# A fused cross-attention, self-attention and expert kernel: self-attention with compact probabilities, scores for the 32x32 diagonal blocks alone, and counters per bank

## What is computed

```python
x = x + xattn(layernorm(x), ctx, Wq, Wk, Wv, Wo, gq, gk)   # 16 heads of 128, 257 keys a sequence
x = x + attn(layernorm(x), w_qkv, w_proj, q_gain)          # the layer that is changed
x = x + moe(layernorm(x), Wg, W1, W3, W2, sw1, sw3, sw2)   # 8 experts, top 1, one shared
# attn: 16 query heads and 4 key heads of 16, ternary weights, a root mean square norm and
# rotary embedding on q and k, causal softmax over the 32 tokens of a sequence, a root mean
# square norm of y over its 256 numbers, then the projection w_proj:
qkv = ternary_linear(x, w_qkv)
q, k = apply_rotary_emb(rms_norm(q)), apply_rotary_emb(rms_norm(k));  q = q * q_gain
y = softmax(causal(q @ k.T * 16 ** -0.5)) @ v
out = ternary_linear(rms_norm(y.reshape(..., 256)), w_proj)
```

## Time and profile before

| | |
|---|---|
| runs | 1604.68, 1611.82 (median), 1613.89 us |
| profiled execution | 1609.09 us; 1607.3 us from the first to the last instruction |
| busy in it | TensorE 1378.4 us (86%), VectorE 1044.2 (65%), ScalarE 864.9 (54%), GpSimd 540.7 (34%) |
| granted TensorE clock, mean | 0.946 |

### The profile page before, as it was taken

One profiled execution on the slowest core, in us unless ns is written; L12 is line 12 of the kernel. 1 busy time (PEld: TensorE's weight loads), 2 busy tenths in 40 slices (PEclk: granted clock), 3 DMA queues, 4 the chain that ended last, 5 costly groups with the idle time before them and its releaser, 6 DMA issues.

```text
span 1607.3 us, 32866 instructions
## 1 busy us (share of the span) xinstructions
PE 1378.4 (86%) x9178; PEld 956.8 (60%) x9178; DVE 1044.2 (65%) x3905; ACT 864.9 (54%) x3432; POOL 540.7 (34%) x1338
## 2 busy tenths in 40 slices
PE   5859989998989898989999998989898989955882
PEld 2635757565756666665757565756666665734661
DVE  6836767676767676777767676767676777733112
ACT  5455656566565656565565566565656565621110
POOL 2143333334243525243343334342525243300003
PEclk9989999999999999999998999999999999976896
DMA  9010000000000001010000000000101010100544
GB/s 372 4 28 8 26 17 21 13 27 13 24 17 14 27 10 30 10 30 7 24 17 21 13 25 15 24 17 10 30 10 30 7 33 3 59 6 19 163 127 134
DMA packets 41190, 59.63 MB, mean 37 GB/s; under 512 B 5094, under 2 KB 35953, under 8 KB 40096
## 3 DMA queue, kind: packets, MB, share of 16 engines
q1 hardware_dynamic: 36880, 50.73, 9.9%
q0 software_dynamic: 2064, 6.14, 1.2%
q10 hardware_dynamic: 2176, 2.10, 0.4%
HBM read 48.62 MB, written 10.49 MB: 37 GB/s over the span
## 4 chain that ended last, share of the span: by engine, by line
PE 57%; issue 14%; POOL 10%; DVE 9%; ACT 7%; DMA 3%; POOLq 1%; SPq 0%; DVEq 0%; ACTq 0%
PE AB L587 30%; PE Eb L587 9%; PE Db L587 5%; PE C L720 3%; PE C L587 3%; ACT px L1003 2%; DMA ctxn<-expert_rows 2%; POOL prob L1140 2%; PE AB L783 2%; POOL c_lo L1105 2%; PE C L704 2%; DVE sc L1509 1%; ACT AB L924 1%; POOL c_hi L1103 1%; POOL pjunk L1099 1%
## 5 line engine op out<-in xcount | busy, mean ns | idle before, releaser
L924 ACT ACTIVATE AB<-AB 128x128 f32<-128x128 f32 (+1 forms) x1160 | 302.8, 261 | 180.8 <-PE AB L587 175.8
L1099 POOL TENSOR_TENSOR pjunk<-pjunk 128x1 f32<-128x1 f32 x288 | 55.9, 194 | 703.2 <-DVE sinv L1443 341.3
L1281 DVE BATCH_NORM_STATS2 kst<-AB 128x6 f32<-128x256 f32 x512 | 182.1, 417 | 71.3 <-PE AB L587 64.9
L587 PE MATMUL AB<-wk_hi,c_hi 128*128 128x512 f16 x512 | 205.2, 401 | 20.8 <-DVE sc L1509 10.0
L924 ACT ACTIVATION_READ_ACCUMULATOR AB<-AB 128x1 f32 (+1 forms) x1160 | 215.4, 186 | 0.0
L587 PE MATMUL AB<-wk_lo,c_hi 128*128 128x512 f16 x512 | 204.0, 398 | 0.0
L587 PE MATMUL AB<-wk_hi,c_lo 128*128 128x512 f16 x512 | 203.0, 396 | 0.0
L993 ACT ACTIVATE prob<-prob,nbias,rq 128x257 f32<-128x257 f32 x256 | 150.6, 590 | 39.8 <-DVE nbias L1438 39.4
L1140 POOL TENSOR_SCALAR prob<-prob,sinv 128x257 f32<-128x257 f32 x256 | 123.8, 484 | 20.1
L587 PE MATMUL AB<-ctxT,qpT 128*128 128x257 f32 x512 | 127.3, 392 | 0.2 <-DVE kst L1281 0.2
L962 ACT CAST pT<-C 128x1024 f16<-128x1024 f32 x64 | 64.5, 1008 | 80.4 <-PE C L720 80.4
(11 more groups left out here) (253 smaller groups left out, 3240.7 us busy)
## 6 DMA issues: line engine op xcount, KB each, us to landing
ctxT<-in_ctxT SPq DMA_DIRECT2D x64, 128.5 KB, 2.1
ctxn<-in_ctxn SPq DMA_DIRECT2D x64, 128.0 KB, 2.1
wq_hi<-in_w SPq DMA_DIRECT2D x4, 768.0 KB, 4.9
wq_lo<-in_w SPq DMA_DIRECT2D x4, 768.0 KB, 6.2
expert_rows<-base POOLq DMA_DIRECT2D x1, 2048.0 KB, 15.7
xin<-in_x SPq DMA_DIRECT2D x16, 128.0 KB, 2.2
prob<-in_wqT SPq DMA_DIRECT2D x1, 2048.0 KB, 19.1
xres<-in_x SPq DMA_DIRECT2D x16, 128.0 KB, 2.0
```

Of the source, the lines that this page charges most:

```text
L587: return pe.matmul(out, lhsT, rhs, start=start, stop=stop)
L924: ins = nc.scalar.activation(k, k, ACT.Square, accum_out=sums[0:m, h:h + 1])
L1099: own.mark(pool.tensor_tensor(pjunk[:, 0:1], pjunk[:, 1:2], pjunk[:, 1:2], ALU.mult))
L1281: ins = V.bn_stats(stats[:, 0, 2 * half + n], AB[0:m, 2 + half, 2 * D * n:2 * D * (n + 1)])
```

## The change

- Scores: 64 products of 32 by 32 (one for each head and sequence), each on its own part of the array by rows and columns, into the first 128 columns of the four banks of `AB`; TensorE first waits for all of the banks (`sc_open` and `pv_open` are counters that nobody waits for). The mask is one operation a bank.
- One exponential of 128x512 into `ex`. New step `sm` on VectorE: sums, reciprocal, product, and a transpose of 32x32 blocks into `exT`. `pt` and its drains go.
- `pv`: 16 products of 32 by 32 rows and 128 columns into the four banks, which give y already transposed, padded from 16 to 32 rows a head; ScalarE copies it to `yT` and squares it; `ys` on VectorE adds the squares, `st` is a product with ones that sums over partitions, `yv` scales. `yt` goes. `pr` has four products, with `wproj` padded (`wpad`, at the start).
- `C` becomes two slots `4` and `5` with counters of their own: `rk`, `pt`, `qk`, `up` fill and drain bank by bank, the drains are two operations for one.
- `o{b}` takes the high halves' products first and waits for the low halves behind them, `f` and `Q` likewise.
- `newton` has one operation less. The clearing of `px` on GpSimd goes.
- The order lists of all four engines are written anew.

```diff
-    "PE": """K0 pt3 K1 K2 X K3 o3 Q f rk0 K4 xt1 K5 qkv QP K6 qk s0 rk1 sc K7 s1 pt pv pt0 s2 yt pr rk2 o0 pt1
-              xt2 s3 lg up pos o1 rk3 pt2 dn o2""".split(),
-    "ACT": """K0 ph3 K1 K2 X tl3 K3 oh3 Q K4 xt1 K5 qkv rk0 QP K6 qk e0 rk1 K7 sc pt e1 ph0 tl0 yt rk2 tl1 ph1 oh0
-              xt2 e2 up oh1 lg rk3 ph2 tl2 e3 oh2""".split(),
-    "DVE": """K0 X K1 dp3 K2 XL K3 do3 KN0 Q RQ f K4 K5 qkv K6 s0 sc K7 i0 s1 pt KN1 pv dp0 i1 pr ln2 s2 dp1 lg i2
-              do0 up pos do1 s3 dn dp2 i3 do2""".split(),
-    "POOL": """h2 h0 h3 h1 n3 X r0 ln1 cl r1 c0 c2 c1 n0 r2 y n1 ln2 c3 r3 n2 scat""".split(),
+    "PE": """K0 K1 pt3 K2 X K3 o3 Q f K4 rk0 xt1 K5 qkv QP K6 qk s0 rk1 sc s1 K7 pt0 pv s2 st pr rk2 o0 pt1 o1
+              xt2 s3 lg up pos rk3 dn pt2 o2""".split(),
+    "ACT": """K0 K1 ph3 K2 X K3 tl3 oh3 Q K4 rk0 xt1 K5 qkv QP K6 qk rk1 e0 sc K7 e1 tl0 pv ph0 rk2 oh0 ph1 tl1
+              xt2 oh1 e2 lg up rk3 ph2 tl2 e3 oh2""".split(),
+    "DVE": """K0 X K1 K2 dp3 XL K3 KN0 Q do3 RQ f K4 K5 qkv K6 s0 i0 sc s1 sm K7 KN1 ys yv i1 dp0 pr ln2 do0 dp1
+              s2 lg do1 i2 up pos s3 dn dp2 do2 i3""".split(),
+    "POOL": """h1 h0 c2 n3 h2 X c3 r0 cl ln1 c0 h3 r1 n0 c1 r2 y n1 ln2 r3 n2 scat""".split(),
...
-SLOTS = {"f": "D", "xt1": "E", "qkv": "D", "qk": "C", "sc": BANKS, "pt": BANKS, "pv": "E", "yt": "D",
-         "pr": "E", "X": "E", "xt2": "D", "Q": BANKS, "lg": "D", "up": "C", "QP": BANKS, "pos": "D", "W0": BANKS, "W1": BANKS,
-         "dn": "E", "M01": BANKS, "M23": BANKS, "tw": "012", "KL": BANKS, "rkl": "C"}
+SLOTS = {"f": "D", "xt1": "E", "qkv": "D", "qk": "45", "sc": BANKS, "pv": BANKS, "st": "D",
+         "pr": "E", "X": "E", "xt2": "D", "Q": BANKS, "lg": "D", "up": "45", "QP": BANKS, "pos": "D", "W0": BANKS, "W1": BANKS,
+         "dn": "E", "M01": BANKS, "M23": BANKS, "tw": BANKS, "KL": BANKS, "rkl": "4"}
 for _b in range(NB):
-    SLOTS |= {f"rk{_b}": "C", f"s{_b}": BANKS, f"pt{_b}": "CD", f"o{_b}": "E"}
+    SLOTS |= {f"rk{_b}": "45", f"s{_b}": BANKS, f"pt{_b}": "45D", f"o{_b}": "E"}
...
-        wproj = sb("wproj", [P, KC, DIM])
+        wproj = sb("wproj", [P, 4, DIM])
...
-        vals = sb("vals", [P, AKV, AD + 1])
+        vals = sb("vals", [P, AKV, SQ])
...
+        ex, wpad, ysq, yred = px[:, 0:4], px[:, 8:16], px[:, 4:8], px[:, 8]
+        exT, yT = pxT[:, 0:4], pxT[:, 4:8]
...
+                for tt, s in enumerate("45"):
                     pe.wait_ge(drained[s].sem, drained[s].turn(p, f"pt{b}"))
-                for tt in range(KT):
                     for g in range(G):
                         ins = pe.transpose(C[:, tt, P * g:P * (g + 1)], prob[:, b, g, P * tt:P * (tt + 1)], ident)
-                ins.then_inc(filled["C"].sem, 1)
+                    ins.then_inc(filled[s].sem, 1)
+                pe.wait_ge(drained["D"].sem, drained["D"].turn(p, f"pt{b}"))
...
                 for tt in range(KT):
+                    pe.wait_ge(ph_ready[tt].sem, ph_ready[tt].at(p, f"ph{b}"))
                     mm(Eb[:], cn_hi[:, b, tt], pT[:, b % 2, 0, tt], start=tt == 0, stop=False)
+                    mm(Eb[:], cn_lo[:, b, tt], pT[:, b % 2, 0, tt], start=False, stop=False)
+                for tt, s in enumerate("45"):
+                    pe.wait_ge(drained[s].sem, drained[s].at(p, f"pt{b}"))
                     mm(Eb[:], cn_hi[:, b, tt], pT[:, b % 2, 1, tt], start=False, stop=False)
-                    mm(Eb[:], cn_lo[:, b, tt], pT[:, b % 2, 0, tt], start=False, stop=False)
+                pe.wait_ge(drained["D"].sem, drained["D"].at(p, f"pt{b}"))
                 mm(Eb[:], cl_rows[:, b], pTl[:, b % 2], start=False).then_inc(filled["E"].sem, 1)
             def step_f(p):
-                pe.wait_ge(drained["E"].sem, drained["E"].at(p, "o3"))
+                pe.wait_ge(oh_ready.sem, oh_ready.at(p, "oh3"))
                 start(p, "f")
                 for h in range(H):
-                    for n, (o, w) in enumerate(((0, wvo_hi), (0, wvo_lo), (1, wvo_hi))):
-                        ins = mm(Db[:, 0:DIM], o_halves[:, o, h], w[:, h], start=(h, n) == (0, 0), stop=(h, n) == (H - 1, 2))
+                    mm(Db[:, 0:DIM], o_halves[:, 0, h], wvo_hi[:, h], start=h == 0, stop=False)
+                    mm(Db[:, 0:DIM], o_halves[:, 0, h], wvo_lo[:, h], start=False, stop=False)
+                pe.wait_ge(drained["E"].sem, drained["E"].at(p, "o3"))
+                for h in range(H):
+                    ins = mm(Db[:, 0:DIM], o_halves[:, 1, h], wvo_hi[:, h], start=False, stop=h == H - 1)
                 ins.then_inc(filled["D"].sem, 1)
...
             def step_sc(p):
-                pe.wait_ge(drained["C"].sem, drained["C"].at(p, "qk"))
-                for m, s in enumerate(BANKS):
+                for s in "45":
+                    pe.wait_ge(drained[s].sem, drained[s].at(p, "qk"))
+                for s in BANKS:
                     pe.wait_ge(drained[s].sem, drained[s].turn(p, "sc"))
-                    rows = slice(32 * m, 32 * m + AD)
...
+                pe.sem_inc(sc_open, 1)
+                for kv in range(AKV):
+                    for b in range(NB):
+                        cols = slice(SQ * b, SQ * (b + 1))
+                        for m, s in enumerate(BANKS):
+                            rows = slice(32 * m, 32 * m + AD)
+                            ins = mm(AB[cols, m, SQ * kv:SQ * (kv + 1)], headsT[rows, kv, cols], headsT[rows, AKV + kv, cols])
+                            if (kv, b) == (AKV - 1, NB - 1):
+                                ins.then_inc(filled[s].sem, 1)
             def step_pv(p):
+                pe.wait_ge(exT_ready.sem, exT_ready.at(p, "h"))
                 start(p, "pv")
-                for n, s in enumerate(BANKS):
-                    pe.wait_ge(drained[s].sem, drained[s].at(p, "pt"))
-                    for h in range(4 * n, 4 * n + 4):
-                        ins = mm(Eb[:, (AD + 1) * h:(AD + 1) * (h + 1)], pxT[:, h], vals[:, h % AKV])
+                pe.sem_inc(pv_open, 1)
+                probs = exT.rearrange("p i (kv q) -> p i kv q", kv=AKV)
+                for kv in range(AKV):
+                    for b, s in enumerate(BANKS):
+                        rows = slice(SQ * b, SQ * (b + 1))
+                        ins = mm(AB[SQ * kv:SQ * (kv + 1), b, 0:P], vals[rows, kv], probs[rows, :, kv])
+                        if kv == AKV - 1:
+                            ins.then_inc(filled[s].sem, 1)
+            def step_pr(p):
+                for s in BANKS:
+                    pe.wait_ge(drained[s].sem, drained[s].at(p, "pv"))
+                start(p, "pr")
+                for i in range(4):
+                    ins = mm(Eb[:, 0:DIM], yT[:, i], wproj[:, i], start=i == 0, stop=i == 3)
                 ins.then_inc(filled["E"].sem, 1)
-            def step_yt(p):
...
+            def step_st(p):
+                pe.wait_ge(yred_ready.sem, yred_ready.at(p, "h"))
+                start(p, "st")
+                mm(Db[:, 0:1], yred, ones[:, 0:1]).then_inc(filled["D"].sem, 1)
...
             def probs_high(p, b):
-                act.wait_ge(filled["C"].sem, filled["C"].at(p, f"pt{b}"))
-                nc.scalar.copy(pT[:, b % 2, 0].rearrange("p t n -> p (t n)"), C[:].rearrange("p a n -> p (a n)"))\
-                    .then_inc(ph_ready.sem, 1)
+                for tt, s in enumerate("45"):
+                    act.wait_ge(filled[s].sem, filled[s].at(p, f"pt{b}"))
+                    nc.scalar.copy(pT[:, b % 2, 0, tt], C[:, tt]).then_inc(ph_ready[tt].sem, 1)
...
             def step_sc(p):
                 act.wait_ge(sc_ready.sem, sc_ready.at(p, "h"))
-                act.wait_ge(px_ready.sem, px_ready.before(p))
...
+                nc.scalar.activation(all_of(ex), all_of(sc[:]), ACT.Exp).then_inc(ex_ready.sem, 1)
...
-            def step_pt(p):
-                for n, s in enumerate("01"):
-                    drain(p, "pt", s, pxT[:, 4 * n:4 * n + 4].rearrange("p h n -> p (h n)"), AB[:, n])
+            def step_pv(p):
+                for b, s in enumerate(BANKS):
+                    act.wait_ge(filled[s].sem, filled[s].at(p, "pv"))
+                    ins = nc.scalar.copy(yT.rearrange("p i (b q) -> p b i q", b=NB)[:, b],
+                                         AB[:, b, 0:P].rearrange("p (i q) -> p i q", q=SQ))
+                    ins.then_inc(drained[s].sem, 1)
+                for s in BANKS:
+                    act.wait_ge(drained[s].sem, drained[s].at(p, "pv"))
+                nc.scalar.activation(all_of(ysq), all_of(yT), ACT.Square).then_inc(ysq_ready.sem, 1)
+            def step_qk(p):
+                for n, s in enumerate("45"):
+                    drain(p, "qk", s, all_of(headsT[:, AKV * n:AKV * (n + 1)]), C[:, n])
...
                 v, w = na[0:rows, 0:n], nb_[0:rows, 0:n]
-                step(V.tensor_scalar(w.bitcast(I32), v.bitcast(I32), 1, None, ALU.logical_shift_right))
-                step(V.tensor_scalar(w.bitcast(I32), w.bitcast(I32), -1.0, MAGIC, ALU.mult, ALU.add))
```

(40 more changed lines are left out.)

179 lines of the change are left out of this document (72 added, 107 removed).

## The result

The changed kernel took 1542.04 us, median of 4 runs (1537.42 to 1546.08), against 1609.78 us for the kernel before, measured beside it (4 runs, 1604.68 to 1613.89). The ratio is 0.958 with an interval of 0.953 to 0.963: 68 us faster, where 50 were forecast.

What follows compares the result with a forecast made beforehand. TensorE was taken as the bound. Stages 37.1 + 9.6 + 35.0 = 81.7, with handovers 82.3, 3.1 us less a period: -46 over 15, last tile -4, 1609 - 50 = 1559, stated as 1560; range 1522 to 1605.

Steps and rivals of the forecast that it cites:

- `sc`, 30 ns a record, 3.8 us: Score products on TensorE: 128 records at 30 ns, 3.8 us for 2.7 before, bounds 13 and 53 ns.
- The rival that decides against the change from 60 ns: Small score products do not overlap: 109 ns a record, 14 us, 1712 us in all; chance 0.11 with weaker forms.
- the 53 ns case: Score records cost 53 to 56 ns as the old tiled ones: +3 us a period, 1605, no change; chance 0.10.
- `pv`, 1.5 us: Products of probabilities and values on TensorE: from 3.5 us to 1.5, at best 0.9.
- `s1` 0.4 idle: TensorE follows the masks bank by bank in `s1`, 686.65 to 688.4, with only 0.4 us idle.
- "I add 0.5" for the clock: Half clock expected after `sc`, on `s1` and `K7`, mostly hidden by VectorE's chain: 0.5 us added to the period.
- `pv` waits 1.4 for `kst`: TensorE before `pv` waits for VectorE's stats of `K7`: 1.4 us, the largest new wait.
- Stage C, 37.1: Period from the end of `K6` to the start of `pt2`: 37.1 us, for 37.64 before.
- Stage A, 9.6, with waits of 1.5 before `K1`: From `pt2` to `pt3`: 9.6 us, about as before, with `K1` now inside and waiting 1.5 for its banks.
- Stage B, 35.0 with 0.4 off the wait for `xn1`: From `pt3` to the end of `K6`: 35.0 us for 37.98, losing `K1`'s 2.6 and 0.4 of the wait.
- The last tile, -4: End of the kernel: shorter self-attention steps save about 9, others add 7, a split saves 2: -4 us.
- The rival of few waits and cheap `sc`: New waits (4.6 us) mostly absent, or score products at their lower bound: period 80, 1525 us; chance 0.17.

Runs made afterwards that it cites:

- wide scores: Changed kernel with the 16 score products of 128 columns and ten masks of before: 1571.53 us, ratio 0.9752.
- Masks first: Changed kernel with `i0` moved behind `sc` in VectorE's list: 1508.91 us, ratio 0.9341.
- the filler: Changed kernel plus six unused full-array products of 512 columns where TensorE waits for the masks: ratio 0.9463.
- `do3` early: Changed kernel with `i0` behind `sc` on VectorE, and `do3` put back ahead of `KN0`: ratio 0.9474.
- same-part kernel: Changed kernel with the 64 small score products reordered, four in a row on the same 32x32 part of the array: 1550.2 us, ratio 0.9618.

## Why the prediction was right, and which terms were off

The time is in the range, the sign and the likeliest case are right, and the period is 82.29 for 82.3. That agreement is partly luck: terms of up to 2.5 us were off and cancelled.

- **`sc`, 30 ns a record, 3.8 us.** Mis-sized: 10 ns, 1.28 us, below my lower bound of 13. I scaled the columns by four from the wide products at 53 ns; but those took 88 ns on average (2.81 us for 32), with four row groups only, while the small ones rotate over sixteen parts. With its four masks the edit is worth -1.5 us a period (wide scores) where the products were charged +1.1. The rival that decides against the change from 60 ns is excluded; I gave it and its weaker forms 0.11, and the 53 ns case 0.10. The trace has a row on either side of the rule in the Trainium skill, "TensorEngine Tiling (Array Packing)", Instruction Overhead (some 60 cycles a matmul, an estimate of 25 ns): 24 ns with four products in a row on one part agrees, 10 ns with neighbours on different parts does not. In the first order the narrow products are longer than the wide ones (3.12 for 2.79 us), in the second less than half.
- **`pv`, 1.5 us.** Measured 0.51, below the 0.9 I gave as the best. `pr` at 1.97 (1.94) and `sm`'s one-pass transpose of 0.71 (0.69) were right; `ys` costs 1.02 for 0.69.
- **`s1` 0.4 idle.** Failed: 1.81. I had `e0` end before `sc` did, at 685.4 against 686.15, "so that `i0` is not late". With `sc` at 1.28 TensorE's scores were ready long before `e0`, and `i0` held the masks 1.4 us beyond them. Masks first shows it. The faster product uncovered the wait that my slow one had hidden.
- **"I add 0.5" for the clock.** Failed. The fall came on `s1` and `K7` as said, and a second time on `s2`, which I had not looked for. Half speed took 2.0 us of TensorE's time a period by the filler and 2.4 by masks first, against one fall in the kernel before. Hiding was half right: with the first fall gone and the masks where they were, the filler gained 0.93. The flaw was to look for one fall and to let VectorE's chain hide most of it.
- **`pv` waits 1.4 for `kst`.** Right: 1.48, and 0.25 once the masks come first. `s2` 0.4: 0.43. `st` 0.7: at most 0.7, and mostly hidden by the slow `s2`; at full clock it is 1.1.
- **Stage C, 37.1.** Measured 36.34 (657.04 to 693.38); 35.4 in the one period where the fall behind `sc` did not come. The 2.5 and 1.0 saved on `sc` and `pv` went into the wait for the masks and the clock.
- **Stage A, 9.6, with waits of 1.5 before `K1`.** Its length is right, 9.59; its parts are not. `K1` hardly waits for ScalarE; instead `K0` waits 0.69 for GpSimd's `c_lo` and `o2` 0.62 for `dn`'s drain. The wait of 1.96 before `o2` and the 1.10 before `pt2` ended as forecast. But the argument was incomplete: it named `dn` as cover for `rk3`'s drains, and the runs show that in the changed lists `dn` and `K1` cover GpSimd's `n2` and `n3` (1.49 and 2.17 without them), 3.3 us a period in all, and the early start of `o` 3.0.
- **Stage B, 35.0 with 0.4 off the wait for `xn1`.** Failed. Measured 36.1: `xn1` waits 1.71 us for 1.1 (means over 14 periods 1.76 and 1.04). In the period before, `f`'s last product was issued by 639.7, but VectorE took the sum at 642.30, behind `RQ`, which ended at 642.28. Both kernels wait for `RQ` there. The changed one has `do3`, 0.67 us, between `Q` and `RQ`, and one step of the roots takes 1.01 to 1.15 for 0.17 beside GpSimd's `cl`; together they eat what the shorter roots gave (from the first step to the last, 3.5 to 3.9 us for 2.92). GpSimd's new list I had costed at nothing, by its idle time alone.
- **Costed at nothing: `f` and `Q` on the high halves first.** No wait stands before either in the trace; no run takes these edits out, so their price is not shown.
- **The last tile, -4.** Mis-sized: about -12, 9.0 from `qk` to the experts and 3.0 beyond a usual period's gain before it. I let `sc`, `sm`, `pr` and the square add 7; `sc` alone took 3.6 off.

By size: the loop gave 50.1 in 14 periods (43 forecast), the end 20 (7 with the fifteenth period). The rival of few waits and cheap `sc` (a period of 80) was half right: `sc` was below its bound, but the waits were there. Without the one of them that `i0` made, the period is 79.55.

## What to carry to other kernels

Before an edit makes one engine faster, look at the step queued ahead of its consumer: here a reciprocal of four columns, in front of four cheap masks, cost 2.7 us a period, with 3.6 gained. Where TensorE is the bound, count a wait beside small-array products as the wait plus what of the half-speed products behind it no other wait covers; moving one entry of another engine's list was worth more than narrow scores and masks (1.5). Start products on the operand that is ready first and put independent products in front of what comes late, then measure each alone: these two were worth 3 us a period each in this kernel's lists, and did not replace one another. Look at the clock in every period, not in one: with `do3` early it fell in 12 of 14, and one of the other two shows nothing of it. And an engine with idle time is not free to run anywhere: GpSimd's `cl` held up VectorE's small steps.

## What the runs showed of the hardware

- fp32 products of 16 rows, 32 columns of weights and 32 columns of data took 10 ns a record (128 in 1.28 us; 256 in 2.34) when neighbours used different parts of the array, 24 ns when four in a row used the same part (3.12 us). Products of 32x32 weights and 128 columns took 16 ns a record (32 in 0.51).
- The granted clock went to 0.50 after such products with idle time behind them (664 to 668; in 13 of 14 periods), and also behind 3.1 us of them with none (583.6 in the same-part kernel; 13 of 14); it stayed at 1.00 behind them in all 14 periods when 1.3 us of full-array products stood between, or when only 0.34 us of idle did. With 256 of them (2.34 us) and no wait of that kind it fell in 7 of 14.
- A 32x32 block transpose of 128x512 fp32 on VectorE took 0.71 us, one pass as for an elementwise operation; a sum over four slices read with a stride took 1.02 us, where one along the row took 0.68.
- VectorE's small steps (8 or 16 columns) took 0.17 us, but 0.5 to 1.15 when a GpSimd operation of 12x512 ran beside them, and ended 0.03 to 0.04 us after it: one a period in the changed kernel, three with `do3` early.
